# Moving the weighted sums and the side tasks between a step's two score groups

## The chip, the cores and the metric

One NeuronCore of a Trainium2 chip runs the whole program. The metric is the device time of one execution in microseconds (us), the median of several executions. TensorE (PE in the profile, PEld for its weight loads), ScalarE (ACT), VectorE (DVE), GpSimd (POOL) and the DMA queue of SyncE (SP) work in parallel and meet at semaphores; each of them executes its own instructions in program order.

## The reference

The input is 8 images of 32x32 positions with 128 channels, in fp32. Two layers follow each other.

```python
# layer 0, for each image (1024 tokens, 8 heads of 16)
qkv = (layernorm(x) * ln_scale + ln_bias) @ w_qkv + b_qkv
attn = softmax(q @ k.T * 16 ** -0.5)         # 1024 x 1024 for each head
x = x + (attn @ v) @ w_out + b_out
# layer 1, for each image
tokens = x @ Win + b_in
q, k, v = heads(layernorm(tokens) @ Wq, Wk, Wv)
pk, pv = 4x4 average pools of k, v           # 64 positions
keep the 16 positions with the largest maximum score; attend to them
tokens += attention; tokens += gelu(layernorm(tokens) @ Wf1 + bf1) @ Wf2 + bf2
out = tokens @ Wout + bout
```

The 8 x 8 matrices of 1024 x 1024 attention scores of layer 0 are most of the work.

## The kernel before

Attention of layer 0 is the backbone. An image n has 32 steps (`STEPS`): 4 pairs of heads times 8 tiles of 128 keys (`TILES`). In a step s, TensorE computes two score groups, `scores(n, s, 0)` and `scores(n, s, 1)` (L643, each two matmuls of 128 keys by 512 queries, one for each head of the pair), for the two halves c of the queries. Each group fills one half of the PSUM tensor `S`. ScalarE takes the exponential of 128x1024 numbers of each group (`exps`, L921) into one of three buffers of `Pr`. TensorE then multiplies by the values, `weighted(n, s)` (L658, eight matmul instructions), accumulating in the PSUM bank `O`. I call this the sums of step s. The waits are these:

- group (s, c) overwrites the half of `S` that the exponential (s-1, c) reads, so it waits for that exponential to end;
- exponential (s, c) waits for its group, and for c = 0 also for the sums of step s-3, which free the buffer of `Pr`;
- the sums of step s wait for both exponentials of step s; the first sums of a head pair also wait until VectorE has turned the bank `O` of the pair before (`divide_o`, L1147).

All other work hangs on these steps by tables written out by hand. `tasks(s)` gives TensorE the projections of the next image (`before_tasks`, the tables `AT_XN`, `AT_Q`, `AT_K`, `AT_V`, `AT_TOKX`, `AT_BOUND`, `AT_FLAG`) and layer 1 of the two images before (`after_tasks`, the tables `USUAL` and `ENDING`). ScalarE and VectorE drain what the tasks leave in PSUM, at the same step numbers: on ScalarE the drains of step s stand behind both exponentials of step s.

In the first image there is no layer 1 yet, and the tasks are: transposes of `xn` (L591) at steps 8 and 10, projections q (17, 19) and k (21, 23) (L596), v (25, 29) (L672), the sums of squares at 28, a flag at 30. In the second image up to step 13 (`LIGHT`) they are `tokx` at steps 0 and 5 and `tok` at 3 (L672), `xn` at 11, the transposes of `that` at 12 (L664) and q of layer 1 at 13 (L691). From step 14 of the second image on there is a task at most steps.

The order on TensorE in one step s of the kernel before is:

- first image: group 0, tasks, group 1, sums of s-1; at s = 0, 8, 16, 24 the tasks stand at the end;
- second image, s < 13: group 0, group 1, sums of s-1, tasks;
- later: group 0, group 1, on even steps the sums of s-2 and s-1, tasks; the last image takes one step's sums at a time again behind step 14 (`FULL`).

Of the kernel before, what the change touches and what calls it, by code (L numbers as in the profile page):

```python
# [33 lines left out]
TILES = T // P  # L34
# [6 lines left out]
STEPS = PAIRS * TILES  # L41
# [16 lines left out]
LIGHT, FULL = 13, 14  # L58
# [6 lines left out]
LAST = IMAGES - 1  # L65
# [16 lines left out]

def sums_behind(n, s):

    if n == 0 or (n == 1 and s < LIGHT) or (n == LAST and s > FULL):
        return (s - 1,) if s > 0 else ()
    return (s - 2, s - 1) if s % 2 == 0 and s > 0 else ()


def tasks_between(n, s):  # L90

    return n == 0 and s % TILES > 0


def xn_steps(n):
# [52 lines left out]
def two_layers(nc, x, ln_scale, ln_bias, w_qkv, b_qkv, w_out, b_out, Win, b_in, Wq, Wk, Wv, g1, be1, g2, be2,  # L148
# [11 lines left out]
    with ExitStack() as ctx:  # L160
# [139 lines left out]
        def wait_for_flag(eng, n):  # L300

            if n == 0:
                eng.wait_ge(first_dve, FIRST_FLAG)
            else:
                eng.wait_ge(a_drained, a_after(n, "flag", 0))
# [255 lines left out]
        def _(pe):  # L561
# [23 lines left out]
            def before_tasks(n, s):  # L585
                if s in xn_steps(n):
                    h = xn_steps(n).index(s)
                    pe.wait_ge(xn_ready, n + 1)
                    a_turn(n, "xn", h)
                    for t in range(4):  # L590
                        mm = pe.transpose(A[:, t * P:(t + 1) * P], xn[:, 4 * h + t, :], ident[:, :])  # L591
                    mm.then_inc(a_filled, 1)
                if s in AT_Q + AT_K:
                    c, h = (0, AT_Q.index(s)) if s in AT_Q else (C, AT_K.index(s))
                    a_turn(n, "k" if c else "q", h)
                    pe.matmul(A[:, :], wqkv_s[:, c:c + C], half(xnT, h), start=True, stop=True).then_inc(a_filled, 1)  # L596
                if s in AT_V:
                    a_turn(n, "v", AT_V.index(s))
                    by_token(A, a_filled, [(xnT, wqkv_s[:, 2 * C:3 * C])], AT_V.index(s))
                if s in AT_TOKX:  # L600
                    a_turn(n, "tokx", AT_TOKX.index(s))
                    by_token(A, a_filled, [(xhT, win_s[:, :])], AT_TOKX.index(s))
                if s == AT_BOUND:
                    pe.wait_ge(squares_ready, n)
                    a_turn(n, "bound", 0)
                    sums_of_squares(A, a_filled)
                if s == AT_FLAG:
                    a_turn(n, "flag", 0)
                    pe.transpose(A[0:1, 0:P], peak[:, :], ident[:, :]).then_inc(a_filled, 1)

            def row_maxima(n):

                for j in range(PAIRS):
                    pe.wait_ge(stack_in[j], 32 + 16 * STACK_DMAS * (n + 1))
                if n > 0:
                    pe.wait_ge(probs_ready, 2 * STEPS * n)
                pe.sem_inc(pe_passed, 1)
                with pe.Fori(0, TILES) as t:
                    pe.wait_ge(tile_copied, TILES * n + t + 1)
                    for h in range(HEADS):  # L620
                        pe.wait_ge(max_drained, MAX_TILES * n + HEADS * t + h + 1)
                        r = 64 * (h % 2)
                        for c in range(2):
                            mm = pe.matmul(S[:, h % 2, c * HALF:(c + 1) * HALF], Qt[r:r + MROW, h // 2, :],
                                           Ks[r:r + MROW, h // 2, c * HALF:(c + 1) * HALF], start=True, stop=True)
                        mm.then_inc(max_filled, 1)
                pe.wait_ge(max_drained, 2 + MAX_TILES * (n + 1))
                pe.sem_inc(pe_passed, 1)
                pe.transpose(S[0:MAX_TILES, 0, 0:P], mx[:, :], ident[:, :]).then_inc(max_turned, 1)
                pe.wait_ge(mneg_ready, n + 1)  # L630
                pe.wait_ge(mrow_in, 16 * HEADS * (n + 1))

            def scores(n, s, c):

                j, kb = s // TILES, s % TILES
                before = 2 * STEPS * n + 2 * s + c - 1
                if before > 0:
                    pe.wait_ge(probs_ready, before)
                if kb == 0 and c == 0:
                    pe.wait_ge(stack_in[j], 32 + 16 * STACK_DMAS * (n + 1))  # L640
                for a in range(2):
                    head = slice(64 * a, 64 * a + MROW + 1)
                    mm = pe.matmul(S[:, c, a * HALF:(a + 1) * HALF], Ks[head, j, kb * P:(kb + 1) * P],  # L643
                                   Qs[head, j, c * HALF:(c + 1) * HALF], start=True, stop=True)
                mm.then_inc(scores_ready, 1)

            def weighted(n, s):

                j, kb = s // TILES, s % TILES
                pe.wait_ge(probs_ready, 2 * STEPS * n + 2 * s + 2)  # L650
                if kb == 0:
                    pe.wait_ge(va_ready, PAIRS * n + j + 1)
                    if n > 0 or j > 0:
                        pe.wait_ge(o_turned, PAIRS * n + j)
                for a in range(2):
                    for c in range(2):
                        r = 32 * (2 * a + c)
                        mm = pe.matmul(O[r:r + 32, :], Va[:, kb, 2 * j + a, :], Pr[:, (STEPS * n + s) % 3, c, a * HALF:(a + 1) * HALF],  # L658
                                       start=(kb == 0), stop=(kb == TILES - 1))
                mm.then_inc(pv_done, 1)  # L660
# [202 lines left out]
            def image(n):  # L863

                wait_for_flag(pe, n)
                pe.sem_inc(pe_passed, 1)
                with pe.If(pe.value_load(flag[0:1, 0:1], min_val=0, max_val=HEADS) > 0):
                    row_maxima(n)
                with pe.Else():
                    pe.sem_inc(max_filled, MAX_TILES)  # L870
                    pe.sem_inc(max_turned, 1)
                def tasks(s):
                    if n > 0:
                        before_tasks(n, STEPS + s)
                    if n + 1 < IMAGES:
                        before_tasks(n + 1, s)
                    if n > 1:
                        after_tasks(n - 2, STEPS + s)
                    if n > 0:
                        after_tasks(n - 1, s)  # L880

                for s in range(STEPS):
                    scores(n, s, 0)
                    if tasks_between(n, s):
                        tasks(s)
                    scores(n, s, 1)
                    for behind in sums_behind(n, s):
                        weighted(n, behind)
                    if not tasks_between(n, s):
                        tasks(s)  # L890
                for behind in sums_behind(n, STEPS):
                    weighted(n, behind)

            image(0)

            pe.wait_ge(weights_in, 16 * WEIGHT_DMAS)
            pe.wait_ge(first_dve, FIRST_DVE)
            for n in range(1, IMAGES):
                image(n)
# [543 lines left out]
```

## Time and profile before

| | us |
|---|---|
| median of 3 executions | 796.75 |
| lowest, highest | 795.85, 799.02 |
| the profiled execution | 800.51 |
| its span, first to last instruction | 798.8 |
| granted TensorE clock, mean over the span | 0.994 of full |

The profile is that of one execution. Its own time is 800.51 us, of which 798.8 us is the span and 1.7 us lies around it. It is 3.8 us above the median. The trace counts time from the start of the span. The first image's attention runs from about 30 to 101 us, the light steps of the second from 102 to 136 us.

### The profile page before, as it was taken

To read this page: it belongs to the slowest core of one execution; us is meant where nothing else is said; L and a number is where in the kernel's file an instruction comes from. 1 tells how busy PE (TensorE), PEld (TensorE's weight loads), DVE (VectorE), ACT (ScalarE), POOL (GpSimd) and SP (SyncE) were. 2 spreads that over 40 slices of the span, in tenths; PEclk is the share of its full clock that TensorE was granted. 3 is DMA by queue.
4 is the path that set the end of the run, shared out by engine and by line. 5 is a ranking of instruction groups with operands and counts; after the bars stand their busy time and mean duration, and the time that the engine had idled before them with its cause. 6 is when DMAs were issued, how large, how long until landed. Compare 5 with 4: busy or idle time off the path is not lost.

```text
span 798.8 us, 14130 instructions
## 1 busy us (share of the span) xinstructions
PE 758.7 (95%) x4973; PEld 360.5 (45%) x4973; DVE 504.5 (63%) x1512; ACT 605.2 (76%) x686; POOL 160.9 (20%) x198
## 2 busy tenths in 40 slices
PE   8889999999999999999999999999999999898977
PEld 4422333345443545345443545345453455233655
DVE  6514445778467675678657775677726784456864
ACT  4598879787887788787897788878887877777313
POOL 2630504320341020410330212410310201100000
PEclk9999999999999999999999999999999999999999
DMA  2544333432443241622523332422414422400100
GB/s 67 104 78 91 63 62 80 91 63 45 81 95 59 48 80 42 132 51 42 98 61 78 61 61 61 116 51 48 76 32 107 67 48 47 112 6 2 34 1 27
DMA packets 44732, 51.32 MB, mean 64 GB/s; under 512 B 15728, under 2 KB 33776, under 8 KB 44656
## 3 DMA queue, kind: packets, MB, share of 16 engines
q1 hardware_dynamic: 44656, 50.35, 32.6%
q8 instruction: 42, 0.69, 0.4%
q14 instruction: 34, 0.28, 0.1%
HBM read 5.45 MB, written 4.19 MB: 12 GB/s over the span
## 4 chain that ended last, share of the span: by engine, by line
PE 59%; ACT 17%; DVE 6%; issue 6%; ACTq 0%; DVEq 0%
PE O L658 20%; PE S L643 15%; ACT Pr L921 12%; PE BC L672 6%; PE BC L790 3%; PE BC L664 2%; PE BC L713 2%; PE BC L772 2%; PE BC L691 2%; PE A L596 2%; ACT hT L970 1%; ACT tT L936 1%; ACT L921 1%; ACT L970 1%; PE A L672 1%
## 5 line engine op out<-in xcount | busy, mean ns | idle before, releaser
L921 ACT ACTIVATE Pr<-S 128x1024 f32<-128x1024 f32 x512 | 493.0, 1029 | 114.0 <-PE S L643 110.2
L658 PE MATMUL O<-Pr,Va 128*32 128x512 f32 x2048 | 253.5, 602 | 1.1 <-ACT Pr L921 0.9
L643 PE MATMUL S<-Qs,Ks 49*128 49x512 f32 x1024 | 217.3, 469 | 18.0 <-ACT Pr L921 16.0
L643 PEld LDWEIGHTS S<-Qs,Ks 49*128 49x128 f32 x1024 | 87.6, 184 | 178.3 <-ACT Pr L921 138.8
L658 PEld LDWEIGHTS O<-Pr,Va 128*32 128x32 f32 x2048 | 50.3, 109 | 105.4 <-issue 97.5
L1147 DVE STREAM_TRANSPOSE OT<-O 128x512 f32<-128x512 f32 x32 | 22.8, 714 | 54.5 <-PE O L658 54.3
L1252 DVE TENSOR_REDUCE r<-BC 128x1 f32<-128x512 f32 x56 | 36.0, 684 | 21.1 <-PE BC L713 21.1
L485 POOL TENSOR_SCALAR xn<-X,ln 128x128 f32<-128x128 f32 x56 | 44.1, 800 | 4.0 <-DVE ln L1060 4.0
L516 POOL TENSOR_TENSOR squares<-qh 128x1024 bf16<-128x1024 f32 x7 | 13.3, 1895 | 154.3 <-DVE hot L1274 117.8
L524 POOL TENSOR_TENSOR q1l<-q1T,q1h 128x1024 fp32r<-128x1024 f32 x7 | 16.7, 2391 | 133.2 <-DVE q1h L1204 133.2
L538 POOL TENSOR_TENSOR tokx<-tokx_new,tok_bias 128x1024 f32<-128x1024 f32 x8 | 18.9, 2362 | 119.1 <-DVE tokx_new L1066 119.1
L507 POOL TENSOR_SCALAR tokx_new<-win_sum,ln 128x128 f32<-128x128 f32 x64 | 37.7, 607 | 1.4 <-POOL tokx L538 1.3
L936 ACT ACTIVATE tT<-BC,cols 128x512 f32<-128x512 f32 x32 | 23.4, 782 | 18.1 <-PE BC L664 18.1
L496 POOL COPY Va<-v_new 128x256 f32<-128x256 f32 x32 | 11.8, 401 | 113.5 <-PE O L658 96.8
L1319 DVE TENSOR_SCALAR hT<-BC,cols 128x512 f32<-128x512 f32 x28 | 21.0, 751 | 18.2 <-PE BC L772 16.7
L596 PE MATMUL A<-xnT,wqkv_s 128*128 128x512 f32 x56 | 31.5, 645 | 0.0
L1328 DVE TENSOR_TENSOR Y<-BC,out_bias 128x512 f32<-128x512 f32 x12 | 8.3, 692 | 34.5 <-PE BC L790 34.5
L772 PE MATMUL BC<-tT,wf_s 128*128 128x512 f32 x56 | 27.5, 614 | 1.1 <-ACT tT L936 0.5
L713 PE MATMUL BC<-Q1s,K1s 96*128 96x512 f32 x56 | 24.3, 516 | 2.2 <-issue 2.2
L790 PE MATMUL BC<-w2o,hT 128*128 128x128 f32 x192 | 24.1, 279 | 0.0
L1154 DVE STREAM_TRANSPOSE On<-OT 128x512 f32<-128x512 f32 x32 | 22.8, 711 | 1.1
L790 PEld LDWEIGHTS BC<-w2o,hT 128*128 128x128 f32 x192 | 22.4, 192 | 2.3 <-issue 2.3
(236 smaller groups left out, 991.3 us busy)
## 6 DMA issues: line engine op xcount, KB each, us to landing
Qs<-qh SPq DMA_DIRECT2D x128, 64.0 KB, 2.3
Ks<-kh SPq DMA_DIRECT2D x128, 64.0 KB, 2.3
Q1s<-q1h SPq DMA_DIRECT2D x56, 128.0 KB, 2.5
X<-in_x_dram SPq DMA_DIRECT2D x8, 512.0 KB, 4.2
Qs<-ql SPq DMA_DIRECT2D x64, 64.0 KB, 2.3
Ks<-kl SPq DMA_DIRECT2D x64, 64.0 KB, 2.3
attnT<-On SPq DMA_DIRECT2D x128, 32.0 KB, 2.0
out_dram<-Y SPq DMA_DIRECT2D x16, 256.0 KB, 2.7
```

What stands on the lines that cost most here:

```text
L485: ins = pool.tensor_scalar(xn[:, t, :], X[:, t, :], ln[:, 0, t:t + 1], ln[:, 1, t:t + 1], ALU.subtract, ALU.mult)
L507: ins = pool.tensor_scalar(tokx_new[:, t, :], win_sum[:, :], ln0[n % 2][:, 0, t:t + 1], None, ALU.mult)
L596: pe.matmul(A[:, :], wqkv_s[:, c:c + C], half(xnT, h), start=True, stop=True).then_inc(a_filled, 1)
L643: mm = pe.matmul(S[:, c, a * HALF:(a + 1) * HALF], Ks[head, j, kb * P:(kb + 1) * P], Qs[head, j, c * HALF:(c + 1) * HALF], start=True, sto ...
L658: mm = pe.matmul(O[r:r + 32, :], Va[:, kb, 2 * j + a, :], Pr[:, (STEPS * n + s) % 3, c, a * HALF:(a + 1) * HALF], start=(kb == 0), stop=(k ...
L672: mm = pe.matmul(bank[:, t * P:(t + 1) * P], lhs[:, c:c + P], w, start=(i == 0), stop=(i == len(pairs) - 1))
L713: pe.matmul(bank[:, :], K1s[0:ROWS1, j, :, :].rearrange("p a b -> p (a b)"), half(Q1s[0:ROWS1, j, :], h), start=True, stop=True).then_inc( ...
L772: pe.matmul(bank[:, :], wf1_s[:, f * C:(f + 1) * C], half(tT, h), start=True, stop=True)\
L790: mm = pe.matmul(bank[:, t * P:(t + 1) * P], hT[:, f, c:c + P], w2o[:, f, :], start=False, stop=(t == 3 and f == 1))
L921: act.activation(Pr[:, g % 3, c, :], S[:, c, :], ACT.Exp, scale=SCALE).then_inc(probs_ready, 1)
L936: act.activation(half(tT, h), bank[:, :], ACT.Identity, bias=be, scale=g).then_inc(drained, 1)
L1252: ins = dve.tensor_reduce(r8[:, 2 * j + h:2 * j + h + 1], bank[:, :], AX.X, ALU.max)
```

## The change

In the first image (all 32 steps) and in steps 0 to 13 of the second, the order on TensorE in a step becomes: group 0, sums of step s-2, tasks, group 1. At the end of the first image the sums of steps 30 and 31 follow. Nothing is added or taken away, no other engine's program is changed, and the rest of the images and the last image's order stay as they are.

```diff
 def sums_behind(n, s):
 
-    if n == 0 or (n == 1 and s < LIGHT) or (n == LAST and s > FULL):
-        return (s - 1,) if s > 0 else ()
+    if sums_between(n, s):
+        return ()
+    if n == 0:
+        return (s - 2, s - 1)
+    if n == LAST and s > FULL:
+        return (s - 1,)
     return (s - 2, s - 1) if s % 2 == 0 and s > 0 else ()
 
 
-def tasks_between(n, s):
-
-    return n == 0 and s % TILES > 0
+def sums_between(n, s):
+
+    return s < STEPS if n == 0 else n == 1 and s <= LIGHT
...
                 for s in range(STEPS):
                     scores(n, s, 0)
-                    if tasks_between(n, s):
+                    if sums_between(n, s):
+                        if s > 1:
+                            weighted(n, s - 2)
                         tasks(s)
                     scores(n, s, 1)
                     for behind in sums_behind(n, s):
                         weighted(n, behind)
-                    if not tasks_between(n, s):
+                    if not sums_between(n, s):
                         tasks(s)
                 for behind in sums_behind(n, STEPS):
                     weighted(n, behind)
```

## Rows read from the trace of the kernel before

**Rows 1.** The page: engines' busy time (share, instructions), and the exponentials' group.

```profile
PE 758.7 (95%) x4973; PEld 360.5 (45%) x4973; DVE 504.5 (63%) x1512; ACT 605.2 (76%) x686; POOL 160.9 (20%) x198
...
L921 ACT ACTIVATE Pr<-S 128x1024 f32<-128x1024 f32 x512 | 493.0, 1029 | 114.0 <-PE S L643 110.2
```

**Rows 2.** Windows: stretch, its length, busy us of each engine, granted clock, DMA.

```profile
30.00:102.00 72.00, 66.56 (x423) 20.97 (x421) 25.46 (x84) 63.51 (x68) 24.92 (x31) 1.00 0.44 78
...
64.00:87.00 23.00, 23.00 (x142) 7.54 (x144) 15.53 (x44) 19.23 (x21) 3.26 (x2) 1.00 0.37 73
...
266.00:697.00 431.00, 420.13 (x2821) 201.31 (x2821) 287.29 (x849) 348.57 (x393) 84.54 (x94) 1.00 0.36 69
```

**Rows 3.** Timeline, first image, steps 2 to 4, no tasks: start, length, engine, line.

```profile
33.93 3.78 ACT L921 ACTIVATE Pr<-S 128x1024 f32<-128x1024 f32 x4 [0.19 <-PE S L643]
...
35.92 0.50 PE L643 MATMUL S<-Qs,Ks 49*128 49x512 f32 x2 [0.19 <-ACT Pr L921]
...
36.35 1.06 PE L658 MATMUL O<-Pr,Va 128*32 128x512 f32 x8
...
37.35 0.92 PE L643 MATMUL S<-Qs,Ks 49*128 49x512 f32 x4
...
37.90 1.94 ACT L921 ACTIVATE Pr<-S 128x1024 f32<-128x1024 f32 x2 [0.18 <-PE S L643]
```

**Rows 4.** Chain that ended last, second image, steps 4 to 6: start, length, what.

```profile
112.98 1.03 ACT Pr L921
...
114.05 0.50 PE S L643
114.55 1.00 PE O L658 x8
115.55 1.09 PE A L672 x8
...
118.03 1.03 ACT Pr L921
```

**Rows 5.** Timeline, first image, steps 18 to 20 and the start of step 26.

```profile
68.56 2.86 ACT L921 ACTIVATE Pr<-S 128x1024 f32<-128x1024 f32 x3 [0.40 <-PE S L643]
...
70.09 1.12 PE L596 MATMUL A<-xnT,wqkv_s 128*128 128x512 f32 x2
...
73.11 1.03 ACT L921 ACTIVATE Pr<-S 128x1024 f32<-128x1024 f32 x1 [0.40 <-PE S L643]
...
86.80 1.03 ACT L921 ACTIVATE Pr<-S 128x1024 f32<-128x1024 f32 x1 [0.40 <-PE S L643]
```

**Rows 6.** Timeline, first image, steps 6 to 11, with the `xn` transposes and drains.

```profile
42.78 1.93 ACT L921 ACTIVATE Pr<-S 128x1024 f32<-128x1024 f32 x2
...
50.47 0.65 PE L591 MATMUL A<-ident,xn 128*128 128x128 f32 x4
...
52.57 0.64 ACT L927 ACTIVATE xhT<-A 128x512 f32<-128x512 f32 x1
...
53.72 3.82 ACT L921 ACTIVATE Pr<-S 128x1024 f32<-128x1024 f32 x4
```

**Rows 7.** Timeline, second image, steps 10 to 14.

```profile
125.02 3.77 ACT L921 ACTIVATE Pr<-S 128x1024 f32<-128x1024 f32 x4 [0.18 <-PE S L643]
...
130.28 1.94 ACT L921 ACTIVATE Pr<-S 128x1024 f32<-128x1024 f32 x2
...
133.04 1.95 PE L691 MATMUL BC<-tT,wq_s 128*128 128x512 f32 x4 [0.26 <-ACT tT L936]
133.42 1.97 ACT L921 ACTIVATE Pr<-S 128x1024 f32<-128x1024 f32 x2
...
135.87 1.92 PE L658 MATMUL O<-Pr,Va 128*32 128x512 f32 x16
```

**Rows 8.** Timeline, second image: layer 0's last output of image 0, layer 1's first input.

```profile
103.37 2.40 SPq L373 DMA_DIRECT2D attnT<-On  x4
...
124.70 2.16 DVE L1163 TENSOR_SCALAR that<-tok,ln 128x128 f32<-128x128 f32 x8
```

## The prediction

> **What bounds the kernel now.** I read the page first. PE is busy 95% of the span, ScalarE 76%, and ScalarE's exponentials sat idle 114 us, nearly all of it waiting for score groups [rows 1]. That average hides two regimes, so I took windows next. From 266 to 697 us TensorE is busy 420 of 431 us and ScalarE 349 [rows 2]: there TensorE's load is the time, and whatever arrives late from the first images is simply added. In the first image ScalarE is busy 63.5 of 72 us and TensorE 66.6: neither is full. But within it, from 64 to 87 us, where the q, k and v tasks lie, TensorE is busy 23.00 of 23.00 us [rows 2].
>
> What sets the pace where neither is full is a loop of waits, which the timeline and the chain show. The building blocks:
>
> - Exponentials behind each other start 0.92 us apart: (3.78 - 1.02) / 3 [rows 3]. One lasts 1.02 to 1.03 us, and a group that waits for its end starts 0.04 us later (112.98 + 1.03, next start 114.05) [rows 4]. So exponential start to group start is 1.07.
> - A group that has waited holds TensorE 0.43 us (35.92 to 36.35), the sums 1.00 us (36.35 to 37.35), and a group's exponential starts 0.55 after the group (37.35 to 37.90) [rows 3].
> - A task's length in the timeline overlaps its successor by about 0.07, as that of the sums does (1.06 against 1.00). q/k tasks hold TensorE 1.05 [rows 5], v and tokx 1.09 [rows 4], the `xn` transposes 0.58 [rows 6].
>
> With no task the loop is: exponential (s,1) ends, group 1 of s+1, sums of s, group 0 of s+2, its exponential, then exponential (s+2,1): 1.07 + 0.43 + 1.00 + 0.55 + 0.92 = 3.97 us for two steps. The trace has 37.90 - 33.93 = 3.97 [rows 3]; ScalarE alone would need 3.68. A task between the sums and the next group lengthens the loop by its length: 112.98 to 118.03 is 5.05 = 3.97 + 1.09 [rows 4].
>
> **The change, part by part.** The new order has the same kind of loop with the halves swapped: exponential (s,0) ends, group 0 of s+1, sums of s-1, task T, group 1 of s+1, its exponential, exponential (s+2,0). It costs 1.07 + 0.43 + 1.00 + T + 0.55 + 0.92 = 3.97 + T for two steps. Nothing is removed; the sums of two steps back have their inputs long ready, but in the kernel before the sums never waited longer than group 1 in front of them, because both wait for the same exponential. So that freedom buys nothing.
>
> (0) Steps without a task, first and second image: 3.97 before and after, 0. Second image, tasks at 3 and 5: sums and task lie in one gap before and after, 3.97 + T both times [rows 4], 0.
>
> (a) First image, steps 8 and 10. ScalarE's two drains stand behind both exponentials of the step and take 53.72 - 52.57 = 1.15 [rows 6]. After: each window of two steps has 3.97 + 0.58 + 1.15 = 5.70, two of them 11.4. Before: the exponential of step 7 starts at 42.78 + 0.92 = 43.70, that of step 11 at 53.72, 10.0 us [rows 6]. Here the task lay in the other gap, and hid. Cost +1.35.
>
> (b) First image, q at 19, k at 21 and 23, v at 25. Before, the pair of steps 18 and 19 takes 73.11 - 68.56 = 4.55 [rows 5]; four such pairs reach from 68.56 to 86.80, 18.24. This is TensorE's load, the gap that the task had for itself having absorbed the rest. After: 3 x 5.02 + 5.06 = 20.1. Cost +1.85. The pair with q at 17 I book at 0, because it comes out of taskless steps with the loop's stall still ahead of it (its upper bound is the 0.46 of the others), and steps 28 to 31 at -0.15, because the new order puts group 1 of a step directly in front of group 0 of the next, which holds TensorE 0.2 less than two groups apart. Their bounds are 0 and -0.2 for each task step.
>
> The first image thus ends 3.05 later; its last sums and the flag's reading between images are as before.
>
> (c) Second image, step 0. The tokx task (1.09) now stands in front of group 1, so the second exponential starts 0.43 + 1.09 + 0.55 - 0.55 = 1.52 after the first and not 0.92: 0.6 late. The stall of 0.3 that the loop had two steps on is swallowed by it. Cost +0.3.
>
> (d) Second image, step 11 (`xn`): 3.97 + 0.58 + 1.15 = 5.70 for what took 130.28 - 125.02 = 5.26 [rows 7]. Cost +0.45.
>
> (e) Second image, step 13, the end of the light stretch. The task (layer 1's q) waits for ScalarE's drain of step 12 and starts at 133.04 at the earliest, before and after, and holds TensorE to 134.92 [rows 7]. Before, both groups of step 13 were ahead of it, and their exponentials ran under it: 133.42 and 134.34. Now group 1 stands behind it: exponential (13,1) starts at 134.92 + 0.55 = 135.47, 1.13 late. Group 1 of step 14 waits for its end, and the double sums of step 14, which started at 135.87 [rows 7], follow that group. From here TensorE is the bound, so the gap stays. Cost +1.1.
>
> Sum: 1.35 + 1.85 - 0.15 + 0.3 + 0.45 + 1.1 = 4.9 us.
>
> What is queued behind the moved instructions: VectorE's `divide_o` waits for the last sums of a pair, which now come about 1.2 us later, so that of step 8 and the normalised `that` behind it end at about 128.1 rather than 126.9 [rows 8]; their reader at step 12 stands behind the `xn` task of step 11, both groups between them and a step's sums, which I place near 129.8, so 0, and 1.2 us of cover are gone. `attnT` is issued by 105.8 and lands some 2 us later [rows 8]; its reader at step 3 stands behind five exponentials, a group and a step's sums, with the image's first exponential near 102.2: 102.2 + 4 x 0.92 + 1.07 + 0.43 + 1.00 = 108.4 at the earliest, so 0. The bank `O` is turned in 0.9 us, the time between two sums in the loop at its shortest; I book 0, at most 0.1 at each of the four pair ends. No DMA moves past another on its queue; they start later with what releases them.
>
> One cost has no direct row: how the sums behind a group that has waited behave when their own inputs are long there. By the nearest rows the first sums cost 1.00 and a second directly behind 1.92 - 1.06 = 0.86 [rows 3, 7], so 0.14 is what their first weight load leaves open. I take 1.00, the row with the same neighbour; the other end, 0.86, would shorten some 22 windows of two steps by 0.14, 3.1 us. The Trainium skill bears on this in "TensorE: Matmul & The Clock Gate", Part 3, "The mechanism": weight loads are pulled ahead of running matmuls only where the row groups differ. Here the sums use all rows, so by it 1.00 stays and the sum is 4.9; by the engine's queue alone, in the same page's table ("pulls LDWEIGHTS ahead of in-flight MATMULs"), it would be 0.86 and 1.8.
>
> **The forecast.** The profiled execution's 800.5 would become 805.4; the same shift on the median gives 796.75 + 4.9 = 801.6 us, +0.6%.
>
> **Rivals.**
>
> 1. The sums' weight load is hidden (above): +1.8, 798.6 us, no measurable change. For: their inputs are ready. Against: they were ready at group 1's start in the kernel before too, and the trace shows 1.00. Chance 0.09.
> 2. The loss is given back later: steps that wait for VectorE or a transfer rather than for TensorE's load take it up. TensorE is idle 11 us in 431 [rows 2]; where this idle time belongs to chains that start from DMA it could absorb 2 to 4 us: 797.6 to 799.6, no change. Against: all those chains start from TensorE's own results. Chance 0.10.
> 3. Not slower but faster: with sums that never wait, the loop breaks and ScalarE runs without stall in the steps without tasks (3.68 for two), while TensorE's load falls by 0.2 per task step. That is some 14 taskless pairs x 0.29 and 9 x 0.2: -5.9 for a loss of at most 1.1 in (e), about 792 us. It decides from where sums and second group fit under the exponentials: sums of at most 0.71 us (1.00 - 0.29). The rows have 1.00. Chance 0.05.
> 4. More than forecast: the cover that is gone in front of `that` or `O` turns into a wait, 1 to 2 us: 803 to 804. Chance 0.10.
>
> The forecast has the remaining 0.66, with its own range of 800.2 to 803.0 (each term by +-30%). The time of this kernel can be told from no change by about 0.5%, 4 us; the forecast's lower edge falls under that, so of its 0.66 about 0.11 counts as same. Slower 0.55 + 0.10 = 0.65; same 0.09 + 0.10 + 0.11 = 0.30; faster 0.05. The range leaves out rival 3, and keeps rivals 1 and 2 in part: 797.8 to 804.0.
>
> **What would show it.** (0) Taskless pairs of the first image still take 3.97, but the stall stands in front of the second exponential. (a) Step 7 to step 11: 11.4. (b) Step 18 to 26: 20.1, each pair 5.0, with TensorE no longer full between 64 and 87 us, but idle about 0.6 per pair in front of group 0. (c to e) The double sums of step 14 of the second image start at about 135.87 + 4.9 = 140.8. The gap between the two traces is then constant to the end. It is wrong if sums behind a waited group hold TensorE clearly under 1.0 us, if a pair with a task takes 4.6, or if the gap shrinks after 141 us.

## The result, and the profile after

The changed kernel takes 802.1 us (median of 4, 801.71 to 803.23) against 796.96 us for the kernel before (4 executions): ratio 1.0059, 95% interval 1.0041 to 1.0077. The forecast was 801.6 us, slower. A second comparison gave more, 1.0094 (1.0074 to 1.0115). Part of what lies between the two goes with the granted clock, which the prediction did not have; that comes below.

The profiled execution of the kernel after took 803.23 us, with a span of 801.5. Its page is that of before in nearly every large group of TensorE and ScalarE [rows 1]. What grew there is the exponentials' idle time, by 3.8 us, and the wait of score groups for exponentials, from 16.0 to 21.4 us:

```profile
span 801.5 us, 14130 instructions
PE 757.5 (95%) x4973; PEld 359.3 (45%) x4973; DVE 504.5 (63%) x1512; ACT 604.9 (75%) x686; POOL 160.6 (20%) x198
...
L927 ACT ACTIVATE Pr<-S 128x1024 f32<-128x1024 f32 x512 | 492.8, 1029 | 117.8 <-PE S L647 116.2
...
L647 PE MATMUL S<-Qs,Ks 49*128 49x512 f32 x1024 | 216.7, 469 | 23.9 <-ACT Pr L927 21.4
```

The same group on the page of before:

```profile
L643 PE MATMUL S<-Qs,Ks 49*128 49x512 f32 x1024 | 217.3, 469 | 18.0 <-ACT Pr L921 16.0
```

Windows of the kernel after answer to [rows 2]. From 64 to 87 us TensorE was full; now it is not, because it waits in front of its score groups. In the middle of the kernel it is as full as before:

```profile
64.00:87.00 23.00, 21.48 (x127) 5.93 (x126) 12.18 (x39) 18.16 (x20) 1.05 (x1) 1.00 0.31 62
266.00:697.00 431.00, 421.92 (x2844) 202.51 (x2843) 287.67 (x849) 350.31 (x396) 84.44 (x94) 1.00 0.35 68
```

The timeline of the kernel after, first image, steps without tasks (answers to [rows 3]):

```profile
33.13 3.78 ACT L927 ACTIVATE Pr<-S 128x1024 f32<-128x1024 f32 x4 [0.18 <-PE S L647]
...
35.13 0.50 PE L647 MATMUL S<-Qs,Ks 49*128 49x512 f32 x2 [0.20 <-ACT Pr L927]
35.55 0.16 PEld L662 LDWEIGHTS O<-Pr,Va 128*32 128x32 f32 x8 [0.24 <-issue]
35.56 1.06 PE L662 MATMUL O<-Pr,Va 128*32 128x512 f32 x8
36.55 0.91 PE L647 MATMUL S<-Qs,Ks 49*128 49x512 f32 x4
37.09 1.94 ACT L927 ACTIVATE Pr<-S 128x1024 f32<-128x1024 f32 x2 [0.18 <-PE S L647]
```

37.09 - 33.13 = 3.96: the loop without a task costs what it did, and the sums, whose inputs are long ready, still hold TensorE 0.99 (35.56 to 36.55). The stall now stands in front of the second exponential of a step.

The same view at steps 19 and 20, where q is computed (answers to [rows 5]):

```profile
70.87 1.06 PE L662 MATMUL O<-Pr,Va 128*32 128x512 f32 x8
71.86 1.12 PE L600 MATMUL A<-xnT,wqkv_s 128*128 128x512 f32 x2
72.92 0.73 PE L647 MATMUL S<-Qs,Ks 49*128 49x512 f32 x4
73.46 2.86 ACT L927 ACTIVATE Pr<-S 128x1024 f32<-128x1024 f32 x3 [1.24 <-PE S L647]
```

Sums and task stand in one gap, and ScalarE is idle 1.24 us in front of the exponential of group 1, where [rows 5] had the task alone in its gap and 0.40 idle.

The end of the light stretch in the second image (answers to [rows 7]):

```profile
136.40 1.96 PE L695 MATMUL BC<-tT,wq_s 128*128 128x512 f32 x4 [0.18 <-ACT tT L942]
...
138.28 0.73 PE L647 MATMUL S<-Qs,Ks 49*128 49x512 f32 x4
138.83 1.02 ACT L927 ACTIVATE Pr<-S 128x1024 f32<-128x1024 f32 x1 [0.99 <-PE S L647]
...
139.90 0.49 PE L647 MATMUL S<-Qs,Ks 49*128 49x512 f32 x2 [0.89 <-ACT Pr L927]
140.33 1.92 PE L662 MATMUL O<-Pr,Va 128*32 128x512 f32 x16
```

Group 1 of step 13 starts behind the task at 138.28, its exponential at 138.83, and group 1 of step 14 waits for that.

So far the forecast. One thing in this trace was not in it. This is the timeline of the kernel after around steps 9 and 10 of the first image:

```profile
47.65 2.86 ACT L927 ACTIVATE Pr<-S 128x1024 f32<-128x1024 f32 x3
...
48.73 0.50 PE L647 MATMUL S<-Qs,Ks 49*128 49x512 f32 x2 [1.54 <-ACT Pr L927]
49.17 1.57 PE L662 MATMUL O<-Pr,Va 128*32 128x512 f32 x8
50.67 1.12 PE L595 MATMUL A<-ident,xn 128*128 128x128 f32 x4
...
52.55 1.02 ACT L927 ACTIVATE Pr<-S 128x1024 f32<-128x1024 f32 x1 [2.04 <-PE S L647]
```

and these are its windows there (length, busy us of each engine, granted clock, DMA):

```profile
46.00:48.00 2.00, 1.20 (x10) 0.19 (x2) 1.09 (x3) 2.00 (x4) 0.33 (x1) 1.00 0.49 78
48.00:50.00 2.00, 1.26 (x10) 0.34 (x10) 1.02 (x2) 2.00 (x3) 0.00 (x0) 0.90 0.37 60
50.00:52.00 2.00, 2.00 (x10) 1.00 (x8) 0.00 (x0) 0.51 (x1) 0.00 (x0) 0.50 0.19 29
```

TensorE idles 1.54 us while ScalarE works through its late exponential and both drains. After that the granted clock is 0.50 (1.2 of 2.4 GHz), the sums take 1.57 instead of 1.06 and the transposes 1.12 instead of 0.65. The kernel before idles 0.61 us at this place and 0.58 us at the next such place, and keeps the full clock.

Distances between the first exponentials of steps, in us, from the trace of each kernel. A stretch of lower clock lengthens the distance that it falls in, so these come from traces that have none there:

| from step to step | before | new order | difference | predicted |
|---|---|---|---|---|
| first image, 7 to 11 (a) | 10.03 | 11.39 (second trace of the kernel after; 12.64 in the first, at the lower clock) | +1.36 | +1.35 |
| first image, 16 to 18, q | 5.04 | 5.00 | -0.04 | 0 |
| first image, 18 to 26 (b) | 18.25 | 20.06 | +1.81 | +1.85 |
| first image, 28 to 31 | 7.19 | 6.91 | -0.28 | -0.15 |
| first image, 31 to second image, 0 | 4.24 | 4.49 | +0.25 | 0 |
| second image, 0 to 4 (c) | 9.88 | 10.18 | +0.30 | +0.3 |
| second image, 10 to 12 (d) | 5.27 | 5.68 | +0.41 | +0.45 |
| second image, 12 to 14 (e) | 5.90 | 7.07 | +1.17 | +1.1 |
| second image, 14 to third image, 0 | 48.97 | 48.89 | -0.08 | 0 |

The differences listed add to 4.9. The distances between step 0 and step 31 of the first image and step 14 of the second that are not listed differ by 0.04 us at most.

The spans of the two profiles differ by 2.7 only. Half-rate stretches fall differently in every execution: the profile before has one in the setup (24 to 28 us, granted 0.57 over the window) and one near 698 us. The first exponential starts 1.7 us earlier after than before, and the last image's 31 steps, in which the second of these stretches lies, take 1.7 us less; the profile after has the stretch of 50 us instead, which cost it 1.2. 4.9 - 1.7 - 1.7 + 1.2 is 2.7. That is why one profile against one profile doesn't give the result here.

### The profile page after: what moved, and what is told of

It reads as the page before. It is cut to its first block, busy times and chain, and to the rows that moved or that the text cites. A ratio compares the mean times of both kernels' runs of the same rounds, so it can differ in the third digit from the quotient of the medians.

```text
span 801.5 us, 14130 instructions
## 1 busy us (share of the span) xinstructions
PE 757.5 (95%) x4973; PEld 359.3 (45%) x4973; DVE 504.5 (63%) x1512; ACT 604.9 (75%) x686; POOL 160.6 (20%) x198
## 4 chain that ended last, share of the span: by engine, by line
PE 65%; ACT 19%; issue 7%; DVE 7%; SPq 1%; DMA 0%; POOL 0%; ACTq 0%; DVEq 0%; POOLq 0%
PE O L662 23%; PE S L647 17%; ACT Pr L927 13%; PE BC L676 6%; PE BC L794 3%; PE BC L668 2%; PE A L600 2%; PE BC L717 2%; PE BC L776 2%; PE BC L695 2%; PE A L676 1%; PE A L595 1%; ACT hT L976 1%; ACT tT L942 1%; ACT L927 1%
## 5 line engine op out<-in xcount | busy, mean ns | idle before, releaser
L647 PE MATMUL S<-Qs,Ks 49*128 49x512 f32 x1024 | 216.7, 469 | 23.9 <-ACT Pr L927 21.4
L662 PEld LDWEIGHTS O<-Pr,Va 128*32 128x32 f32 x2048 | 50.3, 109 | 105.6 <-issue 98.8
L528 POOL TENSOR_TENSOR q1l<-q1T,q1h 128x1024 fp32r<-128x1024 f32 x7 | 16.7, 2388 | 136.0 <-DVE q1h L1210 136.0
```

## The experiments

All timed kernels ran beside the kernel before on the same chip. The mean granted clock of every execution of theirs is known, so besides the ratio I give the difference at equal clock: one fit over 152 executions, those of the table and of the kernel before beside them and the four of the kernel after from the first comparison, with an offset for each kernel and one slope for all. The slope says that 0.01 less of mean clock costs 4.7 us, and what is left scatters by 0.8 us. The 95% intervals of the offsets are +-0.5 to +-0.7 us, +-0.9 for the first comparison.

| kernel | median us | ratio (95% interval) | mean clock, beside before | us at equal clock |
|---|---|---|---|---|
| first image alone | 802.65 | 1.0045 (1.0028 to 1.0061) | 0.9908, 0.9925 | +3.1 |
| second image alone | 802.09 | 1.0056 (1.0034 to 1.0078) | 0.9892, 0.9925 | +2.6 |
| after, tasks behind group 1 in the first image | 800.71 | 1.0022 (1.0007 to 1.0037) | 0.9919, 0.9925 | +2.0 |
| the same in both images | 797.24 | 0.9976 (0.9959 to 0.9993) | 0.9928, 0.9925 | -1.5 |
| after, again | 805.51 | 1.0094 (1.0074 to 1.0115) | 0.9902, 0.9935 | +5.7 |
| after, layer 1's q behind group 1 | 804.70 | 1.0083 (1.0066 to 1.0099) | 0.9897, 0.9935 | +4.5 |
| after, `xn` behind group 1 | 801.98 | 1.0051 (1.0034 to 1.0067) | 0.9930, 0.9935 | +3.5 |
| order searched step by step | 795.31 | 0.9966 (0.9948 to 0.9983) | 0.9936, 0.9935 | -2.5 |
| after, idle time filled | 802.62 | 1.0051 (1.0033 to 1.0070) | 0.9928, 0.9932 | +3.9 |

The kernel after of the first comparison has +4.6 at equal clock, with a mean clock of 0.9948. The first four rows were measured beside each other, so were the next four, and the last stands by itself. Two further kernels, which leave out part of the sums, ran once each and serve for their traces alone: 804.59 us at a mean clock of 0.991, and 803.95 us at 0.977.

### The new order in one image alone

```diff
 def sums_between(n, s):
 
-    return s < STEPS if n == 0 else n == 1 and s <= LIGHT
+    return n == 0 and s < STEPS
```

with the second image's sums as in the kernel before; and the reverse, the first image as before.

> The new order in the first image alone; the second image as in the kernel before. By the terms of the prediction: +3.0 us against the kernel before (1.35 for the xn steps, 1.85 for q, k and v, -0.15 for the last steps), and nothing from the second image. The rival in which the clock matters (the profile after has a half-rate stretch at 49.6 to 53.0 us, behind 1.5 us of idle TensorE at 47.2) expects +3.0 and up to 1.3 more in executions that have such a stretch in the first image.

> The new order in steps 0 to 13 of the second image alone; the first image as in the kernel before. By terms c, d and e: 0.3 + 0.45 + 1.1 = +1.9 us against the kernel before. A theory in which all of the loss belongs to the first image expects 0.

Both parts cost, so a theory that puts all of the loss into the first image falls. At equal clock the first image gives +3.1 (forecast 3.0) and the second +2.6 (forecast 1.9; the trace's own distances give 0.30 + 0.41 + 1.17 = 1.9, and the 0.7 above it are slightly more than the fit's +-0.6 and not explained). The second image's kernel measured +3.4 (by the medians) to +4.3 (by the means) as it ran, with a mean clock 0.0033 below before's, which is worth 1.6 us. Its trace has a half-rate stretch at 105.6 us, where before has none, and that of the first image's kernel has one at 57 us. The window of the kernel with the first image changed:

```profile
56.00:60.00 4.00, 3.41 (x18) 0.89 (x21) 0.00 (x0) 2.72 (x4) 0.00 (x0) 0.64 0.56 100
```

and that of the kernel with the second image changed:

```profile
104.00:108.00 4.00, 3.21 (x14) 0.95 (x16) 0.74 (x3) 3.07 (x4) 0.00 (x0) 0.70 0.18 39
```

### The tasks out of the sums' gap

```diff
                         if s > 1:
                             weighted(n, s - 2)
+                    if tasks_between(n, s):
                         tasks(s)
                     scores(n, s, 1)
...
-                    if not sums_between(n, s):
+                    if not tasks_between(n, s):
                         tasks(s)
```

with `tasks_between` true in the second image's light steps alone, and in a second kernel nowhere.

> The kernel after, but in the first image the tasks stand behind group 1: group 0, sums of s-2, group 1, tasks. Sums two steps back stay in front of group 1, so if the sums' new place costs anything, it costs it here too. My theory is that only sums and tasks in the same gap cost: the first image is then as before (+0.1) and the whole is +1.9 to +2.0, from the second image alone. The rival that the sums' new place costs by itself expects +4 or more.

> The kernel after with the tasks behind group 1 in both images: group 0, sums of s-2, group 1, tasks. The mirror of the kernel before's first image, and in the second image a gap for the tasks of their own, which the kernel before does not give them. By the loops of the prediction: first image +0.1, second image -1.1 (the loss of 0.6 at the start, the xn step and the step with layer 1's q gone), in all -1.0 us against the kernel before: 795.9. The rival that the order of the gaps does not matter in the second image expects 0.

The sums are still those of two steps back and still stand in front of group 1. Yet the first image costs next to nothing: from its step 7 to step 0 of the second image that kernel takes 58.57 us and the kernel before 58.49, and the whole is +2.0 (forecast 1.9 to 2.0). So the sums' new place is free and the shared gap is the cost. With the tasks apart in the second image too, the kernel is faster than before: 0.9976. In its timeline at the q of step 19 the task has its gap, and ScalarE idles 0.4 as in [rows 5]:

```profile
70.33 0.50 PE L652 MATMUL S<-Qs,Ks 49*128 49x512 f32 x2
70.75 1.13 PE L605 MATMUL A<-xnT,wqkv_s 128*128 128x512 f32 x2
71.81 0.49 PE L652 MATMUL S<-Qs,Ks 49*128 49x512 f32 x2
...
73.77 2.85 ACT L933 ACTIVATE Pr<-S 128x1024 f32<-128x1024 f32 x3 [0.41 <-PE S L652]
```

Steps 18 to 26 take 18.24 us there. The second image's light steps, from its step 0 to step 14, take 32.9 us, where before has 34.0: the forecast 1.1 less. The whole is 1.5 less at equal clock (forecast 1.0).

### The kernel after, again, and two of its terms alone

```diff
+def tasks_between(n, s):
+
+    return sums_between(n, s) and not (n == 1 and s == LIGHT)
```

and, for the `xn` steps, `not (n == 0 and s in AT_XN_SECOND)`, in the loop of the experiment above.

> The kernel after, unchanged, for more executions of it beside the kernel before. From the sum of the prediction: +4.9 us where the mean granted clock is the same; the first-image and second-image parts measured alone gave +3.2 and +2.6 at equal clock, which would add to +5.8. The theory that the new order also leaves TensorE more often at the lower clock expects a mean clock below that of the kernel before, and about 1.1 us more for each half-rate stretch of 3.4 us beyond the kernel before's.

> The kernel after, but in step 13 of the second image the task (layer 1's q) stands behind group 1. Term e of the prediction: 1.1 us less than the kernel after, and in the trace 5.9 us from the first exponential of step 12 to that of step 14, as in the kernel before, where the kernel after has 7.07. A theory that the double sums of step 14 are late for another reason (the sums of step 11 now stand in step 13) expects 7.07 to stay.

> The kernel after, but in steps 8 and 10 of the first image the xn transposes stand behind group 1. By the loops each of the two windows loses the 0.58 of the task in its gap: from step 7 to step 11 about 10.2 us as in the run with all tasks apart, where the run of the new order in the first image alone had 11.4. So 1.2 us less than the kernel after. If the half-rate stretch at 49.6 us in the profile after was brought about by the idle time in front of it (1.54 us at 47.2, 0.6 longer than before), it is rarer here; if its place is chance, it is as frequent.

The kernel after came out at +5.7 us at equal clock and at +7.0 as it ran, with a mean clock 0.0033 below before's. That difference is worth 1.6 us by the slope. The +5.7 is 0.8 above the 4.9 of the traces' distances. If the fit gives each of these three groups an offset too, it is +5.3 +-0.8; the rest is not explained.

With layer 1's q behind group 1, steps 12 to 14 of the second image take 5.89 (136.41 to 142.30), as before, where the kernel after has 7.07: term (e) is the place of the task, not the sums of step 11. At equal clock the kernel is 1.2 +-1.0 us below the kernel after (forecast 1.1), 0.8 as it ran. In its timeline both groups of step 13 are ahead of the task, and the double sums start 0.75 behind the end of the task instead of 2.05:

```profile
139.34 1.98 PE L700 MATMUL BC<-tT,wq_s 128*128 128x512 f32 x4
...
141.25 0.82 PE L652 MATMUL S<-Qs,Ks 49*128 49x512 f32 x4
...
142.00 1.92 PE L667 MATMUL O<-Pr,Va 128*32 128x512 f32 x16
```

With `xn` behind group 1, steps 7 to 11 take 10.21 (expected 10.2), and the kernel is 2.2 +-1.0 us below the kernel after at equal clock, 3.5 as it ran: more than the 1.2 of the loops. Its windows at 48 to 60 us hold the full clock:

```profile
48.00:52.00 4.00, 3.25 (x26) 1.13 (x18) 2.11 (x4) 3.80 (x6) 0.00 (x0) 1.00 0.24 38
...
56.00:60.00 4.00, 3.79 (x28) 1.06 (x24) 0.00 (x0) 3.81 (x5) 0.00 (x0) 1.00 0.54 94
```

Those of the kernel after in its second trace don't:

```profile
48.00:52.00 4.00, 2.47 (x18) 0.91 (x18) 2.11 (x4) 3.67 (x5) 0.00 (x0) 1.00 0.26 42
52.00:56.00 4.00, 2.47 (x16) 0.73 (x16) 0.00 (x0) 3.55 (x5) 0.00 (x0) 1.00 0.63 103
56.00:60.00 4.00, 4.00 (x22) 0.89 (x20) 0.00 (x0) 2.66 (x4) 0.00 (x0) 0.57 0.57 103
```

### Idle time filled

```diff
+                    if (n, s) == (0, 8):
+                        pe.wait_ge(first_dve, FIRST_DVE)
+                    if (n, s) in ((0, 10), (0, 12)):
+                        fill(6)
+                    if (n, s) == (1, 2):
+                        fill(1)
                     scores(n, s, 0)
+                    if (n, s) == (1, 1):
+                        fill(3)
```

`fill` issues matmuls of the identity, 128 columns each, into a PSUM bank that nothing uses at that time; the wait at step 8 stands ahead of the first of them.

> The kernel after with extra matmuls of the identity into a free PSUM bank, where TensorE would only wait: six in front of group 0 of steps 10 and 12 of the first image (behind the xn steps, 1.5 us of idle time each), three between the groups of step 1 of the second image and one in front of group 0 of its step 2. They take about 1.3 and 0.7 us and delay the groups by nothing or a tenth. If the idle time brings the half-rate stretches at 50 to 57 us and at 105 to 111 us, both are gone from the trace, steps 9 to 16 of the first image take 15.5 us and the mean is 1 to 2 us below that of the kernel after; at equal clock it is as the kernel after (+4.7 to +5.7). If their place is chance, the trace shows them as before and the mean stays at +6.

The timeline of the filled kernel shows the added work in the gap, 1.60 us of it where 1.3 was expected, and the group behind it on time (1.09 us behind the exponential that it waits for, 1.08 without):

```profile
48.55 1.60 PE L888 MATMUL BC<-ident 128*128 128x128 f32 x12
49.06 2.86 ACT L939 ACTIVATE Pr<-S 128x1024 f32<-128x1024 f32 x3
50.15 0.49 PE L647 MATMUL S<-Qs,Ks 49*128 49x512 f32 x2
```

Its windows over the same 12 us are at the full clock:

```profile
48.00:52.00 4.00, 4.00 (x32) 2.36 (x28) 2.11 (x4) 3.92 (x6) 0.00 (x0) 1.00 0.23 37
52.00:56.00 4.00, 4.00 (x31) 2.22 (x28) 0.00 (x0) 3.31 (x5) 0.00 (x0) 1.00 0.65 106
56.00:60.00 4.00, 3.81 (x26) 1.08 (x26) 0.00 (x0) 3.82 (x5) 0.00 (x0) 1.00 0.55 96
```

The waits are all still there: steps 7 to 11 take 11.43 and 18 to 26 take 20.10. Steps 9 to 16 take 15.45 us, as forecast, where the kernel after has 16.7 and 16.8 in its two traces. What came back is the clock: the mean is 0.9928 beside before's 0.9932. Over all traces of this study, a stretch below full clock between 45 and 60 us is in all six profiles with the new order at steps 8 and 10, the `xn` transposes in the sums' gap and no filling, and in none of the seven others. In four of the six the clock fell 0.9 to 2.0 us behind the first idle time of 1.5 us, and in two it held there and fell behind the second. Between 103 and 114 us such a stretch is in five of the eight with the new order in the second image and no filling, and in none of the five others. So at the first place the idle time brings the lower clock: it goes when the gap is filled, and when the `xn` transposes are moved. At the second place it goes with the new order, but three of eight traces have no such stretch without filling either, so that the one filled trace without it shows nothing there.

What filling is worth in the whole is less clear. The filled kernel is at 1.0051 of before; the kernel after did not run beside it, and had 1.0059 in one comparison and 1.0094 in the other. Against the first the intervals overlap, against the second they do not. At equal clock it was to be as the kernel after, at +4.7 to +5.7, and is at +3.9 +-0.7: the fit leaves 1 us or so unexplained here too.

### The length of the sums

The loop says that the sums' 1.00 us makes the stall of 0.3 in taskless steps, and that 0.71 would end it. Two kernels left out part of the first image's sums: one head of the pair, and then half of each matmul's queries.

```diff
-                for a in range(2):
+                for a in range(2 if n > 0 else 1):
```

```diff
+                        width = HALF if n > 0 else HALF // 2
-                        mm = pe.matmul(O[r:r + 32, :], Va[:, kb, 2 * j + a, :], Pr[:, (STEPS * n + s) % 3, c, a * HALF:(a + 1) * HALF],
+                        mm = pe.matmul(O[r:r + 32, 0:width], Va[:, kb, 2 * j + a, :], Pr[:, (STEPS * n + s) % 3, c, a * HALF:a * HALF + width],
```

> The kernel after, but in the first image only the sums of one head of the pair are computed (half of the sums' matmuls are left out, so they hold TensorE about 0.5 us). By the loop 1.07 + 0.43 + 0.5 + 0.55 + 0.92 = 3.47, under ScalarE's 3.68: the taskless steps run at 3.68 for two, with no stall. The q and k pairs take 3.97 - 0.5 + 1.05 = 4.5 where the kernel after has 5.02. If instead something other than the sums' length set the 3.97, taskless steps stay at 3.97.

> The kernel after, but in the first image each sums matmul takes half of the queries (256 columns instead of 512; the other half of its output is left out). The run with one head left out did not shorten the sums: four instructions took 1.05 us as eight do. Halving the columns should leave about 0.5 us. The loop is then 1.07 + 0.43 + 0.5 + 0.55 + 0.92 = 3.47, under ScalarE's 3.68: taskless steps of the first image at 3.68 for two and without the stall of 0.2 to 0.3, the q and k pairs at 4.5 where the kernel after has 5.02. A theory that something other than the sums' length sets the 3.97 expects 3.97 and 5.02 to stay.

The first missed its aim. Half of the instructions take as long as all, in the timeline of that kernel:

```profile
35.27 1.05 PE L662 MATMUL O<-Pr,Va 128*32 128x512 f32 x4
```

The taskless steps stayed at 3.95 and the q and k pairs at 5.00, which says nothing for or against, since the sums were not shorter. The second did what it should. Its timeline:

```profile
37.31 9.28 ACT L928 ACTIVATE Pr<-S 128x1024 f32<-128x1024 f32 x10 [0.67 <-PE S L647]
...
41.57 0.64 PE L663 MATMUL O<-Pr,Va 128*32 128x256 f32 x8
```

Sums of 0.57 to 0.64, ten exponentials without a stall, and 3.62 us for two steps (expected 3.68). The q and k pairs take 4.59 instead of 5.02 (expected 4.5); the first of them begins 0.4 us before the clock is full again. The loop's terms are what they were taken for. This kernel also met much more of the lower clock, 0.5 from 52.1 to 72.6 us, where the five other traces with idle times of 1.5 us have 3.4 us of it there:

```profile
45.00:60.00 15.00, 12.07 (x82) 4.47 (x80) 2.11 (x4) 13.46 (x16) 2.30 (x4) 0.74 0.49 81
60.00:75.00 15.00, 14.83 (x76) 4.76 (x74) 3.49 (x6) 11.52 (x12) 0.00 (x0) 0.58 0.40 92
```

Why it lasted so long isn't shown. The idle time in front of it was about that of the others (2.42 of 4 us busy from 48 to 52, the kernel after 2.47 in its second trace), and from 60 to 75 us TensorE was busy 14.83 of 15 us.

### A version that beats both

Shortened:

```python
ORDER = {(0, 8): "0T1a", (0, 9): "0b1aT", (0, 11): "0b1aT", (0, 16): "0b1aT", (0, 20): "0T1a", (0, 26): "0T1b",
         (0, 28): "0bT1", (0, 30): "01bT", (1, 1): "0T1a", (1, 2): "0b1aT", (1, 6): "0T1b", (1, 11): "0T1b", (1, 12): "0T1a"}
for part in ORDER.get((n, s), "0b1T"):   # 0, 1: score groups; T: tasks; a, b: sums up to step s-1, s-2
```

> A version meant to be faster than both: as with all tasks apart (group 0, sums of s-2, group 1, tasks), but in 13 steps the sums are brought forward or put behind, so that a step with a task or with ScalarE's drains finds fewer sums in its way. Carrying the waits of the prediction step by step through the first 48 steps gives 3.4 us less than the kernel before, against 1.0 less for all tasks apart (measured: 1.5 less at equal clock). If the loops are only roughly right at this level, the two are the same.

It is at 0.9966 (0.9948 to 0.9983), the fastest of the study, 2.5 us under the kernel before at equal clock. From the first exponential to that of step 16 of the second image its trace has 108.2 us, before 111.3; neither has a stretch of lower clock there, and the forecast was 3.4 less. Of these 3.1 us 0.3 are given back by the third image, whose first exponential comes 152.42 us behind the very first, before 155.17. Its interval and that of the kernel with all tasks apart (0.9959 to 0.9993) overlap, so that it beats that one is likely and not shown.

## Why the prediction was right

**(0), taskless steps, and the sums' length.** Right: 3.97 before, 3.96 after. The sums kept 1.00 us with inputs long ready. This is also what the Trainium skill's "TensorE: Matmul & The Clock Gate", Part 3, "The mechanism", gives for weight loads into row groups in use; the trace agrees, with 0.99: the sums' first weight load starts at 35.55, 0.01 ahead of their first matmul and 0.42 behind the start of the group in front. Rival 1 falls by the 0.99.

**(a) and (d), tasks with drains behind them.** Right in size, +1.36 and +0.41, and shown for (a) by moving the task out (10.21 us for steps 7 to 11, before 10.03). One reading in (a) was wrong without a cost: in the kernel before only the task of step 10 lay in the other gap, that of step 8 stood behind the sums as the new order has it; the 10.0 us that the term starts from held both. But this is where the prediction missed a term: it counted what the exponentials lose, and not that TensorE would idle 1.5 us twice, 6 us apart. That brings the lower clock, and costs another 1.2 us or so where it happens: 12.64 instead of 11.4 for the four steps in the trace after.

**(b), the q, k, v pairs.** Right, +1.81. The pair that I booked at nothing came at -0.04. TensorE is no longer full from 64 to 87 us, as said, but it idles 0.38 per pair in front of group 0 where the prediction had 0.6: it took the groups to hold TensorE 0.2 less, and in these pairs two of the four stand together before and after (0.73 us for the two), so nothing is saved.

**(c), (e).** Right, +0.30 and +1.17, the second shown by taking that task alone behind group 1; (c) and (d) were moved only together with all others.

**The end of the first image.** Steps 28 to 31 gave 0.28 and not 0.15, and the next distance, 31 to the second image, took 0.25 back: together nothing, so that the term of -0.15 wasn't there. Smaller misses the other way make up for it.

**The sum and where it goes.** The distances add to 4.9, the time was 5.1 above before in the first comparison and 7.0 in the second. That the first came within 0.5 us of the forecast is in part luck: its executions of the kernel after had a mean clock of 0.9948, where no kernel in the table has more than 0.9936, and the ratio of the second comparison would make it 804.5, above the stated 804.0. The gap between the traces stays (rival 2 falls: 48.89 us from step 14 to the third image, 48.97 before, and 412.93 us from there to step 16 of the seventh, 413.18 before; the middle of the kernel is as full as it was). Rival 3 falls, and its condition was right: with sums of 0.6 us the stall is gone. Rival 4, a further wait for VectorE's results of 1 to 2 us, didn't appear: no distance is more than 0.25 us above its term. What came on top was none of the rivals but, in part at least, the clock.

**What stays open.** How often the lower clock is met: the first comparison's four executions of the kernel after had a higher mean clock (0.9948) than the second's six (0.9902), and why is not settled. Which idle time is enough isn't either; only that 0.61 us at step 10 wasn't, nor twice 0.74 in the three kernels with the transposes behind group 1, that 1.5 us once or twice was in six of six, and that 0.9 + 0.4 us at the start of the second image was in five of eight. The offsets at equal clock of single experiments differ from the traces' distances by up to 1.0 us, somewhat more than the fit's uncertainty.

## What to carry to other kernels

Where an engine serves another one through two half-buffers, each step has two gaps; write both loops down from one timeline (wait, group, work in the gap, group, latency) and put each piece of extra work into the gap that has room. Two pieces in one gap lengthen the loop even if the engine has time to spare, and a piece whose inputs are ready earlier gains nothing unless its own wait was on the loop. Count also how long the tensor engine idles in the new order: beyond the wait itself it can cost the clock, and work thrown away in the gap can keep it.

## What the runs showed of the hardware that was not expected

- A TensorE idle time of 1.5 us in an otherwise busy stretch was followed by a granted clock of 0.5 in all six traces that have it unfilled, in four behind the first and in two behind the second such idle time; filling it with useless matmuls kept the clock at 1.00 and took steps 9 to 16 from 16.7 to 15.45 us.
- 0.01 of mean granted clock costs 4.7 us of about 800, over ten kernels; most of the spread between executions of one kernel (795.5 to 802.6 us for the kernel before, 35 executions) is that.
- Two of the four 32-column groups of the array (4 instructions) took 1.05 us, all four (8 instructions) 1.06: the groups run side by side, and leaving half of them out frees nothing. Halving the columns took the sums from 1.06 to 0.64.
